# First attention: where DVE takes the second set of side items of a slot, behind one head's thresholds instead of two

## The chip, the cores and the metric

The kernel runs on one core of a Trainium2 chip. Its time is the device time of one launch in microseconds (us), the median over several runs. The engines have a queue each and work in the order in which their instructions are written: PE (TensorE, matmuls), DVE (VectorE), ACT (ScalarE), POOL (GpSimd) and SP (SyncE, which issues DMAs). They meet at semaphores alone.

## The reference, cut to what matters

The program is a two-layer decoder of six stages (three a layer) on x of 8 batches x 256 tokens x 256. The change touches the first stage, an attention with 4 branches of 16 heads of width 16, whose weights are no softmax: softplus of the scaled scores, masked to the past, then w*sigmoid(c*w) (a Silu), then cut off below a threshold of each head, the sink.

```
    Bv, Tv, C = X.shape
    q = (X @ W_Q + b_Q).reshape(Bv, Tv, H_TOT, DH).transpose(0, 2, 1, 3)
    ...
    q, k = (_rope(q), _rope(k))
    scores = jnp.einsum('bhtd,bhsd->bhts', q, k) * ATTNSCALE
    ...
    w = jax.nn.softplus(scores / jnp.sqrt(key_self)[:, :, None, :])
    causal = jnp.tril(jnp.ones((Tv, Tv), bool))
    w = jnp.where(causal, w, 0.0)
    w = w * jax.nn.sigmoid(SCALE * w)
    sinks = sink_scalars.reshape(1, H_TOT, 1, 1)
    w = jnp.where(w < sinks, 0.0, w)
    total = jnp.sum(w, axis=-1, keepdims=True) + sinks + 1e-06
    ...
    y = jnp.einsum('bntc,ncd->bntd', context, W_O) + W_O_bias[None, :, None, :]
    return y.mean(axis=1)
```

## The kernel before

The 16 heads of a batch are worked on in four quads of four heads (each head in all four branches), so the stage has 32 quads, m = 4b + k for batch b and k = 0 to 3. Each engine runs its own loop over slots, one slot for each m (SPAN, a few empty slots ahead and behind), and this order is written out by hand. I call a slot by its k: slot 0 to slot 3 of a batch.

In the slot of quad m the engines do this:

- PE (loop at L417): score groups 1 and 2 of quad m (L346 scores, L349 adds the mask), score group 0 of quad m + 1, the first set of side items, the sums over the weights of quad m - 1 (L366), and the second set of side items.
- ACT (L472): six softplus instructions of quad m, two for each score group (L455); four Silus, one for each head (L484); in between it takes the sums of quad m - 1 out of PSUM (L462) and turned contexts (L469). Each change between softplus and Silu loads a table (L479, L502).
- DVE (L658): takes the first set of side items, cuts the weights of two heads at their thresholds, takes the second set, and cuts the weights of the other two heads. One head is four instructions of 128x384, one for each branch (L654); the last of the sixteen in a slot raises weights_done, for which PE's sums of the next slot wait.
- POOL (L554): adds up rotated queries and keys and finishes contexts behind DVE's items.

The side items are other work that fills the gaps: projections of later batches (q, k, v), the regrouping of sums of quad m - 2, the norm of the keys, the turn of a finished context and the output projection (out). PE computes an item into a PSUM bank, and DVE (ACT for turn) takes it from there. beside_quad (L227) gives both sets of a slot. The second sets, as DVE sees them: slot 0 the out item of batch b - 2 (from batch 2 on), slot 1 one regroup and the keys' projection k of batch b + 1, slot 2 both regroups and q of batch b + 1, slot 3 the other out item of batch b - 1 (from batch 1 on).

PSUM has eight banks. Quad m uses one half of them (banks_of, L222) for its score groups 0 and 2 and the other for group 1; side items and sums of slot m use the half that group 1 of quad m + 1 will write. So the first scores that PE issues in slot m + 1 (L346, by claim at L320) wait until the side items of slot m are taken, the second set too: for an out item by L646, for k and q by L603, for a regroup by L628. DVE's take of an item waits for PE's result of it.

The table that the slots read, in beside_quad; an entry is kind, batch or quad, part and bank:

```
    b, k = divmod(m, QUADS)
    if k == 0:
        sent = [[("regroup", m - 2, 0, 0), ("regroup", m - 2, 1, 1), ("q", b, 2, 2)], [("out", b - 2, 1, 1)]]
    elif k == 1:
        sent = [[("v", b, 0, 0), ("q", b, 3, 1), ("regroup", m - 2, 0, 2)], [("regroup", m - 2, 1, 1), ("k", b + 1, 0, 2)]]
    elif k == 2:
        sent = [[("turn", b - 1, 0, 0), ("turn", b - 1, 1, 1), ("norm", b + 1, 0, 2)],
                [("turn", b - 1, 2, 1), ("turn", b - 1, 3, 2), ("regroup", m - 2, 0, 3), ("regroup", m - 2, 1, 0),
                 ("q", b + 1, 0, 1)]]
    else:
        sent = [[("regroup", m - 2, 0, 0), ("regroup", m - 2, 1, 1), ("q", b + 1, 1, 2)], [("out", b - 1, 0, 1)]]
```

Of the kernel before, what the change touches and what calls it, by code (L numbers as in the profile page):

```python
# [216 lines left out]
def heads_of(k):  # L217

    return slice(8 * (k // 2) + k % 2, 8 * (k // 2) + 8, 2)
# [7 lines left out]
def beside_quad(m):  # L227
# [14 lines that stand above are left out]
    made = lambda kind, of: 0 <= of < (ALL_QUADS if kind == "regroup" else B)  # L242
    return [[(kind, of, i, banks_of(m) + bank) for kind, of, i, bank in part if made(kind, of)] for part in sent]
# [9 lines left out]
def attention0(nc, norm, x_all, xnT_all, ident, psum, a):  # L253
    with ExitStack() as stack:
# [181 lines left out]
        def _(act):  # L436
# [35 lines left out]
            for m in SPAN:  # L472
# [8 lines left out]
                for j in range(4):  # L481
                    if here:
                        wj = w[:, m % QUAD_RING, j].rearrange("p r t -> p (r t)")
                        act.activation(wj, wj, ACT.Silu, scale=SILU_SCALE).then_inc(silu_done, 1)  # L484
                    if j == 0:
                        for _, b, i, bank in turns[:2]:
                            take_turned(b, i, bank)
                    if before and j == (1 if m % QUADS == 2 else 3):
                        for half in range(2):
                            take_sums(m - 1, half)  # L490
                    if j == 1:
                        for _, b, i, bank in turns[2:]:
                            take_turned(b, i, bank)
# [80 lines left out]
        def _(dve):  # L574
# [73 lines left out]
            def threshold(m, j):  # L648

                dve.wait_ge(silu_done, m * 4 + j + 1)  # L650
                for r in range(BR):
                    part = w[:, m % QUAD_RING, j, r, :]
                    col = r * NH + range(NH)[heads_of(m % QUADS)][j]
                    ins = dve.scalar_tensor_tensor(part, part, sinks[:, col:col + 1], part, ALU.is_ge, ALU.mult)  # L654
                if j == 3:
                    ins.then_inc(weights_done, 1)

            for m in SPAN:  # L658
                here = 0 <= m < ALL_QUADS
                first, last = ([item for item in part if item[0] != "turn"] for part in beside_quad(m))  # L660
                for item in first:
                    take(*item)
                for j in range(2):
                    if here:
                        threshold(m, j)
                for item in last:
                    take(*item)
                for j in range(2, 4):
                    if here:
                        threshold(m, j)  # L670

# [1748 lines left out]
```

## Time and profile before

| | us |
|---|---|
| median of 3 runs (lowest to highest) | 2858.23 (2853.45 to 2860.91) |
| the profiled execution's own time | 2861.12 |
| its span, first to last instruction | 2859.1 |
| PE busy | 2470.4 (86%) |
| DVE busy | 1819.9 (64%) |
| ACT busy | 1550.4 (54%) |
| POOL busy | 787.6 (28%) |
| DVE thresholds of the first attention (L654, 512 instructions) | 343.7 |
| ACT softplus (L455, 192) and Silu (L484, 128) | 185.0 and 181.3 |

The profile is of one execution. The first attention takes the span from about 46 us, where its first scores start, to about 704 us, where the last output is added; after that nothing that the change touches runs. Shares of the whole span mix six stages, so the stage is read by itself. A batch in the middle of it (slot 3 of one batch up to slot 2 of the next) takes about 80 us. In a row of the timeline, several like instructions that follow each other stand as one (x8), with their start and the time from the first start to the last end, and in brackets the idle time of the engine ahead of them and what ended it.

### The profile page before, as it was taken

The numbers are of one execution on the slowest core, as the hardware profiler recorded it, in microseconds if no ns is written. First come the engines' busy times: TensorE is split into PE (matmuls) and PEld (weight loads), VectorE is DVE, ScalarE is ACT, GpSimd is POOL, SyncE is SP. The second block draws the span as 40 slices with busy tenths as digits, with TensorE's granted clock in tenths as the row PEclk, the third lists the DMA queues.
The fourth block names the chain that finished last, engine by engine and source line by source line (L and its number), as shares of the span: only waits on it lengthen the run. The fifth ranks groups of instructions, "written<-read, shape, count | busy, mean of one in ns | idle before, by whom it ended". The sixth has DMA issues, their size and how long they took to land. (4 is left out here: it accounts for less than half of the span.)

```text
span 2859.1 us, 46204 instructions
## 1 busy us (share of the span) xinstructions
PE 2470.4 (86%) x17064; PEld 1925.7 (67%) x17064; DVE 1819.9 (64%) x4128; ACT 1550.4 (54%) x3054; POOL 787.6 (28%) x839
## 2 busy tenths in 40 slices
PE   4787878876859999998899999999789999769998
PEld 2444444444646677776688888888767778558887
DVE  5877778775666665554666666666756565455544
ACT  4887878784534444443555555555555555432221
POOL 1332323231014444444211111110036566500000
PEclk8899999888979999999999999999889999979999
DMA  2000000000121111110100000000100000020000
GB/s 90 1 1 1 1 0 1 1 1 20 52 83 27 27 27 28 32 43 4 45 4 6 6 6 3 1 1 1 69 12 5 5 9 1 18 87 8 8 8 30
DMA packets 87052, 55.33 MB, mean 19 GB/s; under 512 B 54960, under 2 KB 78128, under 8 KB 86320
## 3 DMA queue, kind: packets, MB, share of 16 engines
q1 hardware_dynamic: 86832, 52.39, 6.2%
q8 instruction: 139, 2.28, 0.3%
q14 instruction: 81, 0.66, 0.1%
HBM read 37.69 MB, written 8.39 MB: 16 GB/s over the span
## 5 line engine op out<-in xcount | busy, mean ns | idle before, releaser
L654 DVE SCALAR_TENSOR_TENSOR a_w<-a_w,a_sinks 128x384 f32<-128x384 f32 x512 | 343.7, 738 | 10.9 <-ACT a_w L484 9.9
L1991 POOL TENSOR_SCALAR x_weights<-x_weights,x_sums 128x256 f32<-128x256 f32 x256 | 231.9, 924 | 272.5 <-DVE x_sums L2050 272.5
L1083 POOL TENSOR_SCALAR f_weights<-f_weights,f_sums 128x256 f32<-128x256 f32 x256 | 232.0, 924 | 268.5 <-DVE f_sums L1313 268.5
L455 ACT ACTIVATE a_w<-psum 128x1024 f32<-128x1024 f32 x192 | 185.0, 1023 | 124.6 <-PE psum L349 124.2
L346 PE MATMUL psum<-a_qT,a_kT_half 32*128 32x512 f32 x768 | 140.3, 807 | 129.6 <-DVE a_rot L603 36.5
L1241 ACT ACTIVATE f_weights<-psum,f_negmax 128x256 f32<-128x256 f32 x256 | 117.8, 472 | 211.3 <-DVE f_negmax L1307 211.3
L1577 ACT ACTIVATE a_turned_w_hi<-psum 128x512 fp32r<-128x512 f32 x256 | 139.1, 596 | 152.0 <-PE psum L1487 151.9
L1961 ACT ACTIVATE x_weights<-x_masked_s,x_negmax 128x256 f32<-128x256 f32 x256 | 127.0, 497 | 136.5 <-DVE x_negmax L2042 136.5
L1693 DVE TENSOR_REDUCE a_negmax<-psum 128x1 f32<-128x1024 f32 x128 | 156.6, 1224 | 64.8 <-PE psum L119 60.6
L484 ACT ACTIVATE a_w<-a_w 128x1536 f32<-128x1536 f32 x128 | 181.3, 1479 | 0.4
L1655 POOL TENSOR_TENSOR a_xT_lo<-all_xnT_all,a_xT_hi 128x512 fp32r<-128x512 f32 x56 | 71.5, 1276 | 384.8 <-ACT a_xT_hi L1557 384.8
L1700 DVE TENSOR_TENSOR a_turned_w_lo<-psum,a_turned_w_hi 128x512 fp32r<-128x512 f32 x256 | 163.6, 681 | 0.2 <-ACT a_turned_w_hi L1577 0.2
L117 PE MATMUL psum<-a_turned_w_hi,a_v_hi 128*128 128x256 f32 x512 | 150.1, 293 | 0.5 <-DVE a_turned_w_lo L1700 0.5
L346 PEld LDWEIGHTS psum<-a_qT,a_kT_half 32*128 32x128 f32 x768 | 37.4, 224 | 162.1 <-issue 114.6
L118 PE MATMUL psum<-a_turned_w_lo,a_v_hi 128*128 128x256 f32 x512 | 144.8, 283 | 0.0
L119 PE MATMUL psum<-a_turned_w_hi,a_v_lo 128*128 128x256 f32 x512 | 144.8, 283 | 0.0
L1586 ACT ACTIVATE a_weights<-psum,a_negmax 128x1024 f32<-128x1024 f32 x128 | 143.4, 1120 | 2.3 <-DVE a_negmax L1693 2.2
L349 PEld LDWEIGHTS psum<-a_future,a_ident_r 128*128 128x128 f32 x384 | 69.1, 231 | 101.2 <-issue 97.1
L1487 PE MATMUL psum<-all_ident,a_weights 128*128 128x128 f32 x1024 | 132.6, 272 | 0.5 <-ACT a_weights L1586 0.5
L1487 PEld LDWEIGHTS psum<-all_ident,a_weights 128*128 128x128 f32 x1024 | 119.1, 140 | 17.9 <-ACT a_weights L1586 2.2
L544 POOL TENSOR_TENSOR a_ctxn<-a_ctx,a_vnull 128x256 f32<-128x256 f32 x64 | 44.2, 711 | 278.8 <-DVE a_ctx L628 278.8
L117 PE MATMUL psum<-a_kT_hi,a_qT_hi 128*128 128x512 f32 x256 | 106.6, 416 | 7.9 <-issue 6.9
(355 smaller groups left out, 7212.6 us busy)
## 6 DMA issues: line engine op xcount, KB each, us to landing
f_xnT<-all_xnT_all SPq DMA_DIRECT2D x16, 256.0 KB, 2.3
f_pv_rows<-f_pv SPq DMA_DIRECT2D x8, 512.0 KB, 3.2
f_pv_groups<-f_pv_rows SPq DMA_DIRECT2D x8, 512.0 KB
f_w<-in_f_w SPq DMA_DIRECT2D x2, 2048.0 KB, 10.1
all_x_all<-in_x SPq DMA_DIRECT2D x1, 2048.0 KB, 8.3
x_xnT<-all_xnT_all SPq DMA_DIRECT2D x8, 256.0 KB, 2.3
x_ctxT<-in_x_ctxT SPq DMA_DIRECT2D x8, 256.0 KB, 2.9
f_mix_blocks<-f_mix_rows SPq DMA_DIRECT2D x128, 8.0 KB
```

The source lines that it names most:

```text
L117: pe.matmul(out, lhsT[0], rhs[0], start=start, stop=False)
L118: pe.matmul(out, lhsT[0], rhs[1], start=False, stop=False)
L119: return pe.matmul(out, lhsT[1], rhs[0], start=False, stop=stop)
L346: pe.matmul(psum[:, base + j, :], kT_half[rows[j], k % 2, g, keys], at, start=True, stop=False)
L455: act.activation(to, of, ACT.Softplus).then_inc(softened, 1)
L484: act.activation(wj, wj, ACT.Silu, scale=SILU_SCALE).then_inc(silu_done, 1)
L654: ins = dve.scalar_tensor_tensor(part, part, sinks[:, col:col + 1], part, ALU.is_ge, ALU.mult)
L1083: ins = pool.tensor_scalar(w, w, sums[:, k, h, t:t + 1], None, ALU.mult)
L1487: ins = pe.transpose(psum[:, 4 + half, j * P:(j + 1) * P], weights[u % 2][:, lo:lo + P], ident[:])
L1693: dve.tensor_reduce(negmax[:, u % STAT_RING:u % STAT_RING + 1], psum[:, 2 * (u % 2):2 * (u % 2) + 2, :].rearrange("p a n -> p (a n)"), AX. ...
L1700: dve.tensor_tensor(lo, psum[:, 4 + half, :].rearrange("p (j t) -> p j t", t=P), hi.bitcast(F32), ALU.subtract)\
L1991: ins = pool.tensor_scalar(w, w, sums[:, k, h, t:t + 1], None, ALU.mult)
```

## The change

DVE's loop takes the second set of side items behind the thresholds of the first head of a slot, not behind those of the first two. The number of instructions stays the same on every engine, and so does PE's, ACT's and POOL's order.

```
-                for j in range(2):
-                    if here:
-                        threshold(m, j)
+                if here:
+                    threshold(m, 0)
                 for item in last:
                     take(*item)
-                for j in range(2, 4):
+                for j in range(1, 4):
                     if here:
                         threshold(m, j)
```

DVE's order in a slot 1, where the second set is a regroup (L628, L637, L641) and the keys' projection (L598 to L609), before:

```order
L628 COPY a_ctx<-psum 128x4x4x17
L654 SCALAR_TENSOR_TENSOR a_w<-a_w,a_sinks 128x384 x8
L628 COPY a_ctx<-psum 128x4x4x17
L637 TENSOR_TENSOR a_total<-a_ctx,a_sinks_eps 128x4x4 x2
L641 RECIPROCAL a_total<-a_total 128x8x4
L598 STREAM_SHUFFLE a_swap<-psum 128x512
L603 SCALAR_TENSOR_TENSOR a_rot<-psum,a_bk,a_rope 128x256 x2
L609 SCALAR_TENSOR_TENSOR a_rot<-a_swap,a_bk,a_rope 128x256 x2
L654 SCALAR_TENSOR_TENSOR a_w<-a_w,a_sinks 128x384 x8
```

The regroup and the keys come four threshold instructions earlier; twelve follow them instead of eight. Now:

```order
L628 COPY a_ctx<-psum 128x4x4x17
L654 SCALAR_TENSOR_TENSOR a_w<-a_w,a_sinks 128x384 x4
L628 COPY a_ctx<-psum 128x4x4x17
L637 TENSOR_TENSOR a_total<-a_ctx,a_sinks_eps 128x4x4 x2
L641 RECIPROCAL a_total<-a_total 128x8x4
L598 STREAM_SHUFFLE a_swap<-psum 128x512
L603 SCALAR_TENSOR_TENSOR a_rot<-psum,a_bk,a_rope 128x256 x2
L609 SCALAR_TENSOR_TENSOR a_rot<-a_swap,a_bk,a_rope 128x256 x2
L654 SCALAR_TENSOR_TENSOR a_w<-a_w,a_sinks 128x384 x12
```

DVE's order in a slot 0 up to the first item of slot 1 (L617, the values), where the second set is the out item (L646); slot 3 reads alike. Before (-) and now (+):

```order
 L609 SCALAR_TENSOR_TENSOR a_rot<-a_swap,a_bq,a_rope 128x256 x2
-L654 SCALAR_TENSOR_TENSOR a_w<-a_w,a_sinks 128x384 x8
+L654 SCALAR_TENSOR_TENSOR a_w<-a_w,a_sinks 128x384 x4
 L646 SCALAR_TENSOR_TENSOR all_x_all<-psum,all_x_all 128x256
-L654 SCALAR_TENSOR_TENSOR a_w<-a_w,a_sinks 128x384 x8
+L654 SCALAR_TENSOR_TENSOR a_w<-a_w,a_sinks 128x384 x12
 L617 TENSOR_TENSOR a_v<-psum,a_bv 128x16x16 x2
```

The out item moves ahead of the second head's four thresholds.

## Rows read from the trace of the kernel before

**Rows 1.** Windows: stretch, length, busy us (count) of PE, PEld, DVE, ACT, POOL; clock.

```profile
255.63:336.10 80.47, 64.17 (x404) 37.15 (x404) 63.64 (x120) 64.30 (x64) 24.85 (x28) 0.92 0.00 1
```

**Rows 2.** Waits of the stage: who waited for whom, us in total, times, longest.

```profile
PE psum L346 <- DVE a_rot L603: 36.5, 8, 5.1
PE psum L346 <- ACT a_w L455: 32.5, 11, 4.4
PE psum L346 <- issue: 32.5, 14, 2.9
...
PE psum L346 <- DVE all_x_all L646: 14.9, 6, 2.5
...
PE psum L346 <- DVE a_ctx L628: 5.9, 2, 4.7
```

**Rows 3.** Timeline, batch 3, slot 1 into slot 2: start, us, engine, work.

```profile
310.58 1.89 PE L378 MATMUL psum<-all_xnT_all,a_wk 128*128 128x256 f32 x8
...
315.89 0.72 DVE L598 STREAM_SHUFFLE a_swap<-psum 128x512 f32<-128x512 f32 x1
...
317.52 2.09 PE L346 MATMUL psum<-a_qT,a_kT_half 32*128 32x512 f32 x8 [5.05 <-DVE a_rot L603]
318.77 6.11 DVE L654 SCALAR_TENSOR_TENSOR a_w<-a_w,a_sinks 128x384 f32<-128x384 f32 x8
...
320.80 1.94 ACT L455 ACTIVATE a_w<-psum 128x1024 f32<-128x1024 f32 x2 [5.88 <-PE psum L349]
...
327.69 1.50 PE L366 MATMUL psum<-a_w,a_v 128*32 128x512 f32 x16
```

**Rows 4.** Timeline of DVE, cut to the second head's thresholds, slots 0 and 1.

```profile
295.16 2.19 DVE L654 SCALAR_TENSOR_TENSOR a_w<-a_w,a_sinks 128x384 f32<-128x384 f32 x4
...
312.74 2.19 DVE L654 SCALAR_TENSOR_TENSOR a_w<-a_w,a_sinks 128x384 f32<-128x384 f32 x4
```

**Rows 5.** Timeline, slot 3 of batch 2 over slot 0 into slot 1 of batch 3.

```profile
272.40 3.72 PE L414 MATMUL psum<-a_wo,a_ctxT 128*128 128x256 f32 x16
...
277.94 0.41 DVE L646 SCALAR_TENSOR_TENSOR all_x_all<-psum,all_x_all 128x256 f32<-128x256 f32 x1
...
278.61 1.60 PE L346 MATMUL psum<-a_qT,a_kT_half 32*128 32x512 f32 x8 [2.49 <-DVE all_x_all L646]
...
281.40 1.94 ACT L455 ACTIVATE a_w<-psum 128x1024 f32<-128x1024 f32 x2 [3.00 <-PE psum L349]
...
291.17 3.72 PE L414 MATMUL psum<-a_wo,a_ctxT 128*128 128x256 f32 x16
...
292.97 1.06 ACT L462 ACTIVATE a_sumT<-psum 128x512 f32<-128x512 f32 x2
...
297.27 0.41 DVE L646 SCALAR_TENSOR_TENSOR all_x_all<-psum,all_x_all 128x256 f32<-128x256 f32 x1
...
297.79 1.14 PE L346 MATMUL psum<-a_qT,a_kT_half 32*128 32x512 f32 x8 [2.90 <-issue]
...
299.63 1.94 ACT L455 ACTIVATE a_w<-psum 128x1024 f32<-128x1024 f32 x2 [2.35 <-PE psum L349]
```

**Rows 6.** Windows, columns as in Rows 1, scores of four slots' starts.

```profile
278.61:284.21 5.60, 5.60 (x28) 2.54 (x29) 3.97 (x8) 1.94 (x3) 0.00 (x0) 0.70 0.01 3
297.79:301.84 4.05, 4.05 (x28) 1.93 (x28) 4.05 (x8) 1.94 (x2) 0.00 (x0) 1.00 0.00 0
317.52:324.31 6.79, 6.79 (x28) 3.06 (x29) 6.79 (x10) 1.94 (x3) 3.47 (x4) 0.56 0.00 0
398.87:404.09 5.22, 5.22 (x24) 2.43 (x24) 5.22 (x7) 1.94 (x2) 3.47 (x4) 0.70 0.00 0
```

**Rows 7.** Timeline of DVE, start of slot 3 of batch 2.

```profile
267.63 0.88 DVE L628 COPY a_ctx<-psum 128x272 f32<-128x272 f32 x2 [3.50 <-PE psum L399]
```

**Rows 8.** Timeline of PE, the last slot and the tail behind it.

```profile
670.29 3.72 PE L414 MATMUL psum<-a_wo,a_ctxT 128*128 128x256 f32 x16
...
678.76 4.33 PE L366 MATMUL psum<-a_w,a_v 128*32 128x512 f32 x32 [3.87 <-DVE a_w L654]
```

## The prediction, made blind

> **What bounds the kernel now.** I read the stage by itself, first the windows. In a batch of 80.47 us PE is busy 64.17, ACT 64.30 and DVE 63.64 [rows 1]. No engine is full; each idles about 16 us a batch. So the stage is a ring of engines that wait for each other, and what counts is which wait ends last at each change of slot.
>
> The waits name it. PE's first scores of a slot (L346) wait for DVE's take of the keys (L603, eight times, up to 5.1 us), for the out item (L646, six times) and for a regroup (L628, twice) [rows 2]. Fourteen waits are put down to "issue"; six of these are the starts of slot 1 in batches 2 to 7, and there the timeline shows DVE: the out item starts at 297.27, takes 0.41, and PE goes on at 297.79, 0.11 after its end [rows 5]. Behind PE stands ACT: its next softplus (L455) waits 5.88 us after the start of slot 2, 3.00 after that of slot 0, 2.35 after that of slot 1 [rows 3, 5]. A PE start that comes earlier by less than these waits moves ACT by as much, and with ACT everything behind it.
>
> So three of the four slot changes of a batch (0 to 1, 1 to 2, 3 to 0) are set by DVE's take of the second set. The fourth, 2 to 3, is not: PE's second score group there waits for ACT (of the eleven such waits of 32.5 us) [rows 2], so an earlier first group only waits longer.
>
> **What the change does, part by part.** It moves the second set ahead of the second head's four thresholds. These four start at 312.74 in slot 1 and at 295.16 in slot 0, no POOL work beside them [rows 4]. In slot 0 the out item starts at 297.27 [rows 5], so four cost 297.27 - 295.16 = 2.11 us, which is what the item can gain if PE's result is there.
>
> Slot change 1 to 2. The keys' shuffle starts at 315.89; PE's projection lands at 310.58 + 1.89 = 312.47 [rows 3]. 315.89 - 2.11 = 313.78 is later than that, so the whole 2.11 counts. There are eight such changes (in the last batch a regroup alone, which is the 4.7 us wait on L628 [rows 2], moves the same way): 8 x 2.11 = 16.9.
>
> Slot change 0 to 1. PE's output projection lands at 291.17 + 3.72 = 294.89 [rows 5], before 295.16 [rows 4]: again the whole 2.11, six times (batches 2 to 7, since the out item is missing in the first two): 12.7.
>
> Slot change 3 to 0. The out item starts at 277.94, and PE's result lands at 272.40 + 3.72 = 276.12 [rows 5]. Four thresholds earlier would be 275.83; DVE now waits about 0.3 for PE, and the gain is 277.94 - 276.15 = 1.79, six times: 10.7.
>
> Slot 2. No gain, as said. DVE waits for PE's regroup after one head's thresholds, and the four that it had done by then come behind the item, 2.1 us later. DVE's next work, in slot 3, begins after 3.50 us of idle time [rows 7], which hides them with 1.4 left.
>
> The tail. In the last slot PE's output projection lands at 670.29 + 3.72 = 674.01, and PE's sums behind it wait for the last threshold (3.87 us) [rows 8]. DVE now stands at the out item with twelve thresholds undone instead of eight, and nothing follows that could hide them: four more, +2.1 us.
>
> The later weights_done. Of the thresholds' delay, PE's sums of the next slot are what could wait. In slot 1 DVE's work stays the same in sum, so its last threshold still ends 318.77 + 6.11 = 324.88, while PE's sums, at 327.69 [rows 3], come 2.11 earlier: 0.7 us of cover is left. That is the tightest place. If it goes, each further us there is lost again.
>
> These terms sum to 16.9 + 12.7 + 10.7 - 2.1 = 38.2 us.
>
> **The clock.** PE's idle time before these starts also costs speed. From PE's start to ACT's fifth softplus, the start of slot 0 takes 5.60 us at a granted share of 0.70, that of slot 1 4.05 at 1.00 (2.4 GHz throughout; 0.5 is 1.2 GHz) [rows 6]. At the change 3 to 0 PE idles 2.49 before it [rows 5], and with the change 0.7. I take the clock as held there: 1.55 x 6 = 9.3. The bounds are 0 and that. At the change 1 to 2, PE idles 5.05 now [rows 3] and 2.94 then. The start of slot 2 takes 6.79 at 0.56 in batch 3 and 5.22 at 0.70 in batch 4 [rows 6]; at full clock it could take 4.05. The trace shows both outcomes near 2.94: 2.90 at the start of slot 1 leaves the clock whole, 2.49 at slot 0 does not [rows 5, 6]. Bounds: -0.8 on average (if half of the eight are like batch 4's now and all become like batch 3's) to +2.74 each. I take 0.7, since above it PE meets the late weights_done: 8 x 0.7 = 5.6. Both clock terms make 14.9.
>
> The Trainium skill, "TensorE: Matmul & The Clock Gate", section "HAM oscillation — how this bites in real kernels", says that a matmul stream which waits too long between bursts starts each burst at the low clock. By a rule on the length of a wait alone, 2.90 would be cut before 2.49 is; the rows show the reverse, so here the length alone does not decide, and the sum leaves both outcomes open (38 without the clock, 53 with it).
>
> **Sum.** 38.2 + 14.9 = 53.1 us. The profiled execution took 2861.12, so 2808.0; against the median of the runs, 2858.23, it gives 2805.1. I forecast **2805**.
>
> **The rivals.** (1) The clock gives nothing back: the starts stay at their shares of now, and the shift alone counts: 2858.2 - 38.2 = 2820. For it speaks that a start at 0.70 is seen behind 2.49 us of idle time and that the slot 2 to 3 stays cold anyway; against it that only 0.7 us of idle is left ahead of slot 0.
>
> (2) DVE becomes the bound. By the forecast a batch falls by 2.11 + 2.11 + 1.79 + 1.55 + 0.7 = 8.3 to 72.2 us, and DVE's 63.64 [rows 1] are 88% of that, with its short waits for PE still to add. If the changes 0 to 1 and 1 to 2 then pay half, 38.2 - 14.8 = 23.4 is left and no clock: 2835. For it: 0.7 us of cover in slot 1. Against it: DVE has waits of 3 us and more at the head of three slots, such as [rows 7].
>
> (3) No change. PE, freed of DVE, waits for the next thing that holds its banks, ACT's taking of the sums (L462). In slot 0 these end at 292.97 + 1.06 = 294.03, and the out item now ends at 295.57 [rows 5]: 1.5 us too early to bind. It decides if ACT comes that much later against DVE. Then nothing is gained: 2858. The same time follows if occupancy decided, since no engine loses work. The Trainium skill, "Trace Analysis", section "Identifying the Most-Contended Engine", says to take the engine with the highest occupancy as the bottleneck and to work on that first; the change takes no work from any, so by that rule the time would stay. [rows 1] speak against it: the busiest engine is at 80%.
>
> (4) Slower. DVE, in order, stands before a side item that PE has not finished, with three heads' thresholds behind it; weights_done is late, PE's sums wait, ACT waits for the sums, and the slot is longer. The tail shows the price: 2.1 us. It decides where DVE's new wait is longer than the cover, 0.7 us in slot 1. At all 31 later slots it would be +65, 2923; with the gains of the other changes still there, something like a third of that, 2880, is what could happen. The rows give no new wait over 0.3 us in slots 0, 1 and 3, so it is unlikely.
>
> **How the numbers follow.** Forecast 0.70, (1) 0.17, (2) 0.07, (3) 0.04, (4) 0.02. All but the last two are faster by over 0.3% (8.6 us, about what a measurement of this kernel can tell from no change): 0.94, 0.04, 0.02. The range is to hold 8 in 10. Downwards, the slot 2 starts could keep the full clock for part of what lies beyond 0.7 us, some 1.3 more at each of eight: 2805 - 10 = 2795. Upwards it takes in rival (1) and the loss of 0.8 at eight starts, 2820 + 6, and a little of rival (2): 2828.
>
> **What would show it.** Right: PE's waits for L603 fall from about 5.05 to 2.94 each, the waits at the starts of slots 0 and 1 to 0.7 to 0.8; a batch in the middle falls from 80.5 to about 72 us; the window of scores at the start of slot 0 shows 4.05 us at 1.00; the last sums start 2.1 us later against the last out item; the stages behind are unchanged. Rival (1): the same waits, but a batch of 74.5 us. Rival (2): PE's sums (L366) waiting for L654 in slot 2. Rival (3): PE's L346 waiting for L462. Rival (4): DVE waiting for L414 or L378 in the middle of its thresholds for more than 0.7 us. The forecast is wrong in its base if ACT's waits behind PE do not shrink with PE's.

## The result and the profile after

The changed kernel takes 2807.89 us (median of 6 runs, 2803.09 to 2812.0); the kernel before, in runs beside it, 2861.4 (6 runs, 2853.45 to 2863.48). The ratio is 0.9815, with a 95% interval of 0.9801 to 0.9828. That is 53.5 us less; the forecast was 53.1 less, 2805. All times in this document are of fast runs: one of the five runs of the kernel with slot 1 alone (below) took 2931.21 us at a lower granted clock and is left out of its median.

The profiled execution after took 2803.09 us, the shortest of the six. Its page begins so:

```profile
span 2801.1 us, 46204 instructions
...
PE 2450.8 (87%) x17064; PEld 1915.1 (68%) x17064; DVE 1817.3 (65%) x4128; ACT 1551.4 (55%) x3054; POOL 786.4 (28%) x839
```

The counts are those of before: no engine lost an instruction. To see where the time went, one window is laid over the first attention, from its first scores to the last output that DVE adds. The first row is of the kernel before, the second of the kernel after (columns as in [rows 1]: stretch, length, busy us of PE, PEld, DVE, ACT, POOL with counts, then PE's granted clock):

```profile
46.40:704.43 658.03, 517.21 (x3204) 297.19 (x3204) 496.29 (x933) 512.01 (x501) 192.46 (x218) 0.89 0.00 1
```

```profile
44.87:650.03 605.16, 500.29 (x3204) 290.20 (x3204) 493.93 (x933) 512.65 (x501) 191.30 (x218) 0.92 0.00 1
```

The stage is 52.9 us shorter. PE issues the same 3204 matmuls in both, so its part splits cleanly in two. It is idle for 104.9 us instead of 140.8, that is 35.9 less; this is waiting. And it is busy for 16.9 us less with the same work; this is the clock, granted at 0.92 instead of 0.89. Laid against the granted clock, 122.4 us of PE's busy time before were at 1.2 GHz, and 84.4 after; at full speed 38 us of it take half, which is 19 and covers the 16.9. The forecast had 38.2 and 14.9. The other 5.1 us by which the two spans differ lie outside the stage, where nothing was changed.

The waits of the stage after, answering to [rows 2] (who waited for whom, us in total, times, longest):

```profile
ACT a_w L455 <- PE psum L349: 64.5, 54, 8.5
...
PE psum L346 <- ACT a_w L455: 34.9, 10, 4.7
...
PE psum L346 <- DVE a_rot L603: 21.7, 8, 2.9
PE psum L346 <- issue: 18.9, 14, 2.9
PE psum L366 <- DVE a_w L654: 11.4, 9, 4.9
...
PE psum L346 <- DVE all_x_all L646: 4.3, 6, 0.8
...
PE psum L346 <- DVE a_ctx L628: 3.1, 2, 2.6
```

PE's waits for DVE's take fell at every change of slot that the prediction named: for the keys (L603) by 14.8 us, for the out item (L646) by 10.6, under "issue" by 13.6, for the regroup (L628) by 2.8. Of the 13.6, 12.7 are the six starts of slot 1 (from 2.88 to 2.90 each to 0.76 to 0.78), and of the 2.8, 2.1 are the start of slot 2 in the last batch; nearly all of the rest is ahead of slot 3 in batches 0 and 7. ACT's wait for PE fell with them, to 64.5 us; in the kernel before it was:

```profile
ACT a_w L455 <- PE psum L349: 124.2, 54, 9.1
```

One wait is new: PE's sums (L366) for DVE's thresholds (L654), 11.4 us in nine places where there was one of 3.9 [rows 8]. And one is gone. In the kernel before, the sums of slot 2 waited in seven batches for ACT to take turned contexts:

```profile
PE psum L366 <- ACT a_ctxT L469: 4.3, 7, 1.4
```

The change of slot 1 to 2 in batch 3, answering to [rows 3] (start, us, engine, work, and in brackets the idle time ahead and what ended it):

```profile
294.61 1.89 PE L378 MATMUL psum<-all_xnT_all,a_wk 128*128 128x256 f32 x8
...
297.80 0.73 DVE L598 STREAM_SHUFFLE a_swap<-psum 128x512 f32<-128x512 f32 x1
...
299.43 1.69 PE L346 MATMUL psum<-a_qT,a_kT_half 32*128 32x512 f32 x8 [2.94 <-DVE a_rot L603]
300.69 8.22 DVE L654 SCALAR_TENSOR_TENSOR a_w<-a_w,a_sinks 128x384 f32<-128x384 f32 x12
...
302.31 1.94 ACT L455 ACTIVATE a_w<-psum 128x1024 f32<-128x1024 f32 x2 [3.37 <-PE psum L349]
...
308.97 2.93 PE L366 MATMUL psum<-a_w,a_v 128*32 128x512 f32 x32 [0.50 <-DVE a_w L654]
```

Twelve thresholds now follow the keys, the scores wait 2.94 us instead of 5.05, and ACT's softplus waits 3.37 instead of 5.88. The last row shows the later thresholds: PE's sums, which had found the weights ready [rows 3], now wait 0.50 for the last of the twelve. In this place that costs nothing. Before, the second half of the same sums waited as long for ACT:

```profile
329.68 1.50 PE L366 MATMUL psum<-a_w,a_v 128*32 128x512 f32 x16 [0.49 <-ACT a_ctxT L469]
```

From their first start to their end the sums then took 329.68 + 1.50 - 327.69 = 3.49 us; now the wait and the sums make 0.50 + 2.93 = 3.43.

A batch in the middle, answering to [rows 1], and the scores at the starts of slots 0, 1 and 2 of batch 3, answering to [rows 6]:

```profile
240.00:311.72 71.72, 61.41 (x408) 36.13 (x404) 63.36 (x120) 64.34 (x64) 24.68 (x28) 0.95 0.00 1
...
266.32:270.36 4.04, 4.04 (x28) 1.94 (x28) 4.04 (x9) 2.98 (x4) 0.00 (x0) 1.00 0.02 4
281.81:285.87 4.06, 4.06 (x28) 1.94 (x29) 4.06 (x9) 3.58 (x5) 0.00 (x0) 1.00 0.00 0
299.43:305.02 5.59, 5.59 (x28) 2.54 (x28) 5.59 (x7) 1.94 (x2) 3.48 (x4) 0.69 0.00 0
```

The batch is 71.72 us long instead of 80.47 (forecast 72.2), with DVE and ACT as busy as before. The start of slot 0 now runs at the full 2.4 GHz, 4.04 us instead of 5.60. The start of slot 2 still shows 0.69, a mixture of 1.2 and 2.4 GHz.

The tail, answering to [rows 8]: the last out item that DVE takes in the stage's last slot, the thresholds behind it, and PE's last sums.

```profile
615.77 0.42 DVE L646 SCALAR_TENSOR_TENSOR all_x_all<-psum,all_x_all 128x256 f32<-128x256 f32 x1 [1.00 <-PE psum L414]
616.11 6.43 DVE L654 SCALAR_TENSOR_TENSOR a_w<-a_w,a_sinks 128x384 f32<-128x384 f32 x12
...
622.60 5.23 PE L366 MATMUL psum<-a_w,a_v 128*32 128x512 f32 x32 [4.93 <-DVE a_w L654]
```

From the out item to the sums it is 622.60 - 615.77 = 6.83 us. Before, the out item began at 674.05 and the sums at 678.76, which is 4.71: 2.1 more now, as forecast.

### The profile page after: what moved, and what is told of

It is laid out like the page before. It is cut to its first block and busy times, and to the rows that moved or that the text cites. A ratio compares the mean times of both kernels' runs of the same rounds, so it can differ in the third digit from the quotient of the medians.

```text
span 2801.1 us, 46204 instructions
## 1 busy us (share of the span) xinstructions
PE 2450.8 (87%) x17064; PEld 1915.1 (68%) x17064; DVE 1817.3 (65%) x4128; ACT 1551.4 (55%) x3054; POOL 786.4 (28%) x839
## 5 line engine op out<-in xcount | busy, mean ns | idle before, releaser
L654 DVE SCALAR_TENSOR_TENSOR a_w<-a_w,a_sinks 128x384 f32<-128x384 f32 x512 | 343.0, 739 | 3.5 <-ACT a_w L484 3.5
L455 ACT ACTIVATE a_w<-psum 128x1024 f32<-128x1024 f32 x192 | 185.3, 1023 | 65.0 <-PE psum L349 64.5
L346 PE MATMUL psum<-a_qT,a_kT_half 32*128 32x512 f32 x768 | 127.4, 737 | 90.5 <-ACT a_w L455 34.9
L346 PEld LDWEIGHTS psum<-a_qT,a_kT_half 32*128 32x128 f32 x768 | 34.9, 208 | 121.9 <-issue 69.8
L2287 DVE SCALAR_TENSOR_TENSOR f_acc<-psum,f_p,f_acc 128x256 f32<-128x256 f32 x112 | 54.2, 484 | 89.1 <-PE psum L119 85.7
```

The lines of the kernel that those rows point to most:

```text
L346: pe.matmul(psum[:, base + j, :], kT_half[rows[j], k % 2, g, keys], at, start=True, stop=False)
L455: act.activation(to, of, ACT.Softplus).then_inc(softened, 1)
```

## The experiments

Apart from the fillers below, all of them edit one place, DVE's loop. It thresholds some heads, takes the second set, and thresholds the other heads:

```
+                ahead = <number of heads>
+                for j in range(ahead):
-                for j in range(2):
                     if here:
                         threshold(m, j)
                 for item in last:
                     take(*item)
-                for j in range(2, 4):
+                for j in range(ahead, 4):
```

The kernel before is 2 in every slot, the change is 1 in every slot. In this table a ratio is to the kernel before on the same chip, with its interval. Gains in us are told below as this ratio's share of 2861, since the medians come from several chips and go apart by some us. PE's idle and busy time are of one profiled execution, over the stage as above, less those of before. The forecast's terms, with the same signs, stand in the last column (idle, busy).

| heads ahead of the second set | us | ratio | idle | busy | forecast |
|---|---|---|---|---|---|
| 1 in slot 1 (e1_again) | 2850.79 | 0.9964 (0.9945 to 0.9984) | -12.0 | +1.9 | -16.9, -5.6 |
| 1 in slot 0 (e2_slot0) | 2851.68 | 0.9963 (0.9948 to 0.9978) | -11.8 | -0.3 | -12.7, 0 |
| 1 in slot 3 but the last (e3_slot3) | 2842.86 | 0.9931 (0.9916 to 0.9946) | -11.0 | -7.0 | -10.7, -9.3 |
| 1 in slot 2 (e4_slot2) | 2862.66 | 1.0004 (0.9995 to 1.0014) | +1.2 | -4.3 | 0, 0 |
| 1 in slots 0 and 3 (e10_slots03) | 2832.05 | 0.989 (0.9874 to 0.9907) | -23.1 | -7.3 | -23.4, -9.3 |
| 1 in slots 0, 1 and 3 (e5_013) | 2803.96 | 0.9805 (0.9788 to 0.9821) | -37.8 | -22.5 | -40.3, -14.9 |
| 1 everywhere (the change) | 2807.89 | 0.9815 (0.9801 to 0.9828) | -35.9 | -16.9 | -38.2, -14.9 |
| 0 everywhere (e6_none) | 2823.11 | 0.9867 (0.9849 to 0.9885) | -24.6 | -14.4 | |
| 3 everywhere (e7_three) | 2920.89 | 1.0207 (1.0192 to 1.0222) | +46.2 | +12.6 | |

Lengths of slots, where they are given below, run from ACT's fifth softplus in the slot before to ACT's fifth softplus in the slot itself, so that the wait ahead of a slot's start and that start count as this slot's; sums are over all batches.

How far one execution's clock can be trusted shows in the row of slot 2: the medians are the same, and yet its profiled stage is 3.0 us shorter, with 4.3 of busy time. So a few us of busy time mean nothing here.

### One change of slot at a time

Slot 1 alone:

```
+                ahead = 1 if m % QUADS == 1 else 2
```

> The move in slot 1 of each batch alone (regroup and keys ahead of the second head's thresholds); slots 0, 2 and 3 as before. Theory (the slot changes pay one by one, and the gains add): eight changes of 2.11 us, 16.9, and up to 7 more from the clock at the start of slot 2, so 17 to 24 us less than before, about 2840. PE's wait for L603 falls from 5.05 to 2.94. Rival (the ring takes the gain back elsewhere as long as one slot alone is moved, since another wait comes to stand in its place): under 5 us.

Measured: 2852.16 us (median of 4), ratio 0.9965 (0.995 to 0.9981), about 10 us less, and so too little. The same kernel was run again for its trace.

> The move in slot 1 alone once more, for a profile and a second time: the first gave 10 us (ratio 0.9965), less than the 17 to 24 that were expected, and its profile was of a disturbed run. Theory 1 (the shift of 2.11 us pays eight times, but the clock at the starts of slots 2 and 0 falls otherwise than it did and takes some back): PE's wait for L603 is 2.94 in each batch, the lengths of slot 1 to slot 2 fall by 2.1 or more, and other slot lengths grow. Theory 2 (the shift itself does not pay, PE's sums in slot 2 meet the late thresholds): PE's L366 waits for L654 by about 2 us in slot 2 of each batch. The time again about 2851.

Measured: 2850.79, again about 10 us less. The first two rows are the stage and the start of slot 1 in batch 3, then the starts of slots 2 and 3 in batch 4:

```profile
46.39:694.28 647.89, 519.07 (x3204) 297.89 (x3204) 494.53 (x933) 513.19 (x501) 192.71 (x218) 0.89 0.00 1
```

```profile
295.18:302.15 6.97, 6.97 (x28) 3.19 (x30) 4.12 (x8) 1.95 (x3) 0.00 (x0) 0.54 0.00 0
395.18:399.24 4.06, 4.06 (x28) 1.94 (x29) 4.06 (x5) 1.95 (x3) 3.23 (x4) 1.00 0.00 0
412.77:422.09 9.32, 6.13 (x28) 2.73 (x28) 7.75 (x10) 6.90 (x8) 5.00 (x5) 0.58 0.00 0
```

PE's waits for the keys did fall to 2.93 each, as worked out, and slots 2 are together 24.6 us shorter. But slots 1 are 7.4 longer and slots 3 are 7.7 longer. In three batches the start of slot 1, which took 4.05 before, is now slow (6.97 at 0.54 in batch 3). And where the start of slot 2 runs at the full clock, as in batch 4, the sums meet DVE's late thresholds: PE waits 2.03 us for them in batches 2, 4 and 6, and the start of slot 3 behind them takes 9.32 us at 0.58. So the wait was shortened, but the clock only changed its place, and where a start of slot 2 was fast the cover in slot 1 gave out. The length of the wait does not tell which start is slow: behind the same 2.93 us slot 2 takes 4.06 in batch 4 and 6.95 in batch 3.

Slot 0 alone, and slot 3 alone (without the last slot of all, so that the tail stays):

```
+                ahead = 1 if m % QUADS == 0 else 2
```

> The move in slot 0 of each batch alone (the out item ahead of the second head's thresholds). Theory: six changes of 2.11 us, 12.7 in all, no term of the clock, since the start of slot 1 runs at a share of 1.00 already: about 2849. PE's wait at the start of slot 1 falls from 2.90 to 0.78. Rival (the gain is taken back elsewhere): under 5 us.

Measured: 2851.68 us, about 10.6 less; 11.8 us of idle time are gone and the clock is as it was. The shift is worth what its term said, within 1 to 2 us.

```
+                ahead = 1 if m % QUADS == 3 and m < ALL_QUADS - 1 else 2
```

> The move in slot 3 of each batch alone, the very last slot left as before. Theory: six changes of 1.79 us, 10.7, and six times 1.55 us because the start of the next slot 0 keeps the full clock (5.60 us becomes 4.05): 20.0 in all, about 2841. Rival 1 (the clock gives nothing): 10.7, about 2851, and the window stays at 5.6. Rival 2 (taken back elsewhere): under 5 us.

Measured: 2842.86, about 20 less, as expected. The rows are the starts of slots 0 and 1 of batch 3:

```profile
274.41:278.47 4.06, 4.06 (x28) 1.94 (x28) 4.06 (x9) 3.52 (x4) 0.00 (x0) 1.00 0.02 4
292.03:296.07 4.04, 4.04 (x28) 1.94 (x29) 4.04 (x8) 1.95 (x3) 0.00 (x0) 1.00 0.00 0
```

Slot 0 now starts at full clock behind 0.7 us of idle time, in all six batches, and slot 1 keeps it behind 2.88 in five of them; in batch 6 it starts at 0.69 (5.59 us) behind 2.90. Both terms of this change of slot, shift and clock, came in, less those 1.5 us.

Slot 2 alone:

```
+                ahead = 1 if m % QUADS == 2 else 2
```

> The move in slot 2 alone. Theory (PE's second score group of slot 3 waits for ACT there, so an earlier or later take of the queries moves nothing, and the later thresholds are hidden by 3.5 us of idle time of DVE): no change, 2861, within 3. Rival (the later thresholds or DVE's wait for the regroup cost): 2866 or more.

Measured: 2862.66, ratio 1.0004 (0.9995 to 1.0014): no change. The change of slot 2 to 3 is not set by DVE.

### The changes of slot together

```
+                ahead = 1 if m % QUADS in (0, 3) and m < ALL_QUADS - 1 else 2
```

> The move in slots 0 and 3, not in slots 1 and 2, the very last slot as before. Alone they paid 10.6 and 19.7 us, slot 1 alone 10; all three 57 or so. So some 17 us belong to moves that stand together. Theory (clock: a start that keeps its clock sends the low clock on to the next start that waits long; with slots 0 and 3 moved those starts wait 0.8 us and cannot take it, so slot 1 pays its full 17 to 24 only on top of them): 12.7 + 20.0 = 32 us here, about 2830, and the change adds 24 to that. Rival (slots 0 and 3 help each other, slot 1 pays 10 in any company): 45 us, about 2817.

Measured: 2832.05, about 31 less, the sum of the two alone (10.6 + 19.7). Idle time adds up too: 23.1 against 11.8 + 11.0.

```
+                ahead = 2 if m % QUADS == 2 or m == ALL_QUADS - 1 else 1
```

> The changed kernel with slot 2 and the very last slot as before (second set behind two heads there). Theory: slot 2's move pays nothing and costs nothing, so its return changes nothing; the last slot gives back the 2.1 us of the tail: 2806 against 2808 for the change, a ratio of about 0.981. Rival (slot 2's move has its part in the gain, through DVE's earlier take of the queries): 2812 or more. Second rival (slot 2's move costs, its thresholds being late for PE's sums): under 2803.

Measured: 2803.96, a ratio of 0.9805 where 0.981 was expected. It keeps the changes that pay and leaves out the tail's 2.1 us. The intervals of the two ratios (0.9788 to 0.9821 here, 0.9801 to 0.9828 for the change) overlap, so that it is better than the change is not shown, though it is the fastest of the runs.

What the prediction did not have comes out of the pair. With slots 0 and 3 moved, slot 1 is worth (0.989 - 0.9805) x 2861 = 24 us; alone it was worth 10. The three alone make 10.3 + 10.6 + 19.7 = 40.6 us, together they make about 56. The idle time explains little of that: 12.0 + 11.8 + 11.0 = 34.8 alone, 37.8 together. The busy time explains it: 5.4 us in sum alone, 22.5 together. So the shifts add up, and the clock does not. The expectation of the kernel with slots 0 and 3 had this; its rival, that slot 1 pays 10 us in any company, is out. Busy time at 1.2 GHz, of one execution each, says the same: 122 us before, 127 with slot 1 alone, 107 with slot 3 alone, 105 with slots 0 and 3, 72 with all three.

### The clock by itself

These kernels leave DVE's order alone and give PE something to do ahead of a start: extra matmuls into a bank that the coming scores overwrite, whose results nobody reads. Ahead of slot 0, on the kernel before:

```
                 first, last = beside_quad(m)
+                if here and m % QUADS == 0 and m >= 8:
+                    bank = banks_of(m - 1) + 2
+                    pe.wait_ge(*free[bank])
+                    for _ in range(9):
+                        pe.matmul(psum[:, bank, 0:T], same_head[:], xnT_all[:, 0, 0, :], start=True, stop=True)
```

> The kernel before, with nine extra matmuls of 128x256 (about 2.1 us) that PE does in its idle 2.49 us ahead of slot 0 from batch 2 on, into a PSUM bank that is free then; their result is overwritten. DVE's order is as before, so PE's wait for the out item ends when it did and nothing is shifted. Theory (the idle time there costs clock as well as time): the start of slot 0 takes 4.05 us instead of 5.60 at a granted share of 1.00, six times 1.55 = 9.3 us less, about 2852. Rival (the low clock at this place lies beside other work and costs nothing, or goes on for another reason): no change, 2861.

Measured: 2863.62, ratio 1.0011 (0.9998 to 1.0024). This one was mis-sized: the nine took 3.87 us instead of fitting into the 2.49 us of idle time, and held the scores back by about 1.4, so its time says nothing of the clock. Its trace says one thing: slot 0 starts at full clock in all six batches, and slot 1 is slow behind it in two of them (6.91 and 6.83 us) and fast in four. The filler in batch 3:

```profile
280.28 4.05 PE L424 MATMUL psum<-all_xnT_all,a_same_head 128*128 128x256 f32 x18
```

With five in place of nine:

```
-                    for _ in range(9):
+                    for _ in range(5):
```

> As e8_fill0, with five extra matmuls instead of nine (nine took 3.87 us, not 2.1, and so held back the scores of slot 0 by some 1.4 us each). Five take about 2.15 of the 2.49 us that PE idles. Theory (the idle time ahead of slot 0 costs clock as well): the start of slot 0 takes 4.05 us at full clock at its old place, 6 x 1.55 = 9.3 us less, about 2852. Rival (the low clock there costs nothing on the path): 2861.

Measured: 2860.4, ratio 0.9997 (0.9985 to 1.0008): nothing gained, where 9.3 us were expected. The starts of slots 0 and 1 of batch 3:

```profile
280.61:284.65 4.04, 4.04 (x28) 1.94 (x29) 3.97 (x8) 1.95 (x3) 0.00 (x0) 1.00 0.02 4
298.22:303.81 5.59, 5.59 (x28) 2.54 (x29) 4.12 (x8) 1.94 (x3) 0.00 (x0) 0.69 0.00 0
```

The filler did what it should: slot 0 starts at full clock in all six batches, and slots 0 are 10.8 us shorter. But now slot 1 starts at 0.69 in all six, 5.59 us instead of 4.05; slots 1 are 7.4 longer, and the rest is 2.9 longer. Keeping one start at speed moved the slow start to the next long wait. The term "1.55 x 6" of the prediction is therefore not had by a fast start of slot 0 alone. (The filler is more work for PE, too; no run tells apart whether slot 1 is slow for this work or for the wait.)

Ahead of slot 2, on top of the change:

```
+                if here and m % QUADS == 2 and m >= 2:
+                    bank = banks_of(m - 1) + 3
+                    pe.wait_ge(*free[bank])
+                    for _ in range(6):
+                        pe.matmul(psum[:, bank, 0:T], same_head[:], xnT_all[:, 0, 0, :], start=True, stop=True)
```

> The changed kernel with six extra matmuls (about 2.6 us) in the 2.94 us that PE still idles ahead of slot 2, into a bank that is free then; the result is overwritten. It keeps the clock at the start of slot 2 without shifting PE's start. Theory (the weights' cover is used up: PE's sums in slot 2 already wait 0.5 us for DVE's last threshold, so an earlier ACT meets PE's later sums): the start of slot 2 falls from 5.59 to 4.05 us, PE's wait for L654 in slot 2 grows from 0.5 to about 2 us, and the time falls by less than 4 us, 2804 or more. Rival (the clock is what still costs there): 8 x 1.55 = 12 us less, 2796.

Measured: 2815.95, ratio 0.9848 (0.9831 to 0.9865), about 9 us slower than the change by the ratios. The expectation had up to 4 us of gain and no loss. The start of slot 2 and the sums of that slot in batch 3 as windows, and the sums and ACT's taking of them in the timeline (lines are 5 higher here, so L659 is the threshold):

```profile
301.40:305.46 4.06, 4.06 (x28) 1.94 (x28) 4.06 (x5) 1.94 (x2) 3.23 (x4) 1.00 0.01 4
310.95:315.41 4.46, 4.46 (x33) 1.31 (x34) 2.65 (x5) 2.19 (x3) 0.00 (x0) 0.62 0.00 0
```

```profile
310.95 4.46 PE L366 MATMUL psum<-a_w,a_v 128*32 128x512 f32 x32 [2.04 <-DVE a_w L659]
...
313.80 0.60 ACT L467 ACTIVATE a_sumT<-psum 128x512 f32<-128x512 f32 x1 [1.25 <-PE psum L366]
```

The start gains 5.59 - 4.06 = 1.53 us, and 2.04 - 0.50 = 1.54 of it comes back as waiting for the last threshold. Behind that longer wait the sums run at 0.62, 4.46 us instead of 2.93, and slot 3 is over 3 us longer. In batch 1 the sums keep the full clock, and there slots 2 and 3 together take as long as with the change, within 0.3 us. So the cap that the prediction put on slot 2 is real: a faster start of slot 2 is worth nothing once DVE's thresholds are what the sums wait for, and less than nothing when the wait costs the clock.

### How many heads ahead

```
+                ahead = 0
```

> The second set ahead of all thresholds, in every slot. Theory (from one head to none PE's results are not there yet): DVE waits about 3.9 us for the output projection in slots 3 and 0 (0.3 and 0 behind one head), 1.8 for the keys in slot 1; some of it is won back as POOL's work falls into the wait and no longer beside thresholds; DVE has no slack left at the change 3 to 0 and 1.3 us at 0 to 1; the tail is 2 us longer. 17 to 37 us slower than the change: 2825 to 2845. Rival (only PE's release counts, so earlier is always better): 2806 or less.

Measured: 2823.11, ratio 0.9867 (0.9849 to 0.9885), 15 us slower than the change. The waits of its stage, then DVE at the change of slot 0 to 1 in batch 3:

```profile
DVE all_x_all L646 <- PE psum L414: 64.5, 16, 11.8
...
PE psum L366 <- DVE a_w L654: 36.0, 9, 8.1
...
PE psum L346 <- DVE a_rot L603: 13.4, 8, 1.7
```

```profile
284.10 0.42 DVE L646 SCALAR_TENSOR_TENSOR all_x_all<-psum,all_x_all 128x256 f32<-128x256 f32 x1 [2.24 <-PE psum L414]
284.44 8.54 DVE L654 SCALAR_TENSOR_TENSOR a_w<-a_w,a_sinks 128x384 f32<-128x384 f32 x16
```

This is the slower rival at work: DVE stands before an out item that PE has not finished, 2.24 us here and 3.85 at the change of slot 3 to 0 before it, with all sixteen thresholds behind it, and PE's sums wait 36.0 us for thresholds instead of 11.4. (Of the 64.5 us in the first row, 21.3 are the end of the stage; with the change the row has 25.8 in all.) The time came out a little below the expected range, and the loss was not where it was expected. Slots 0 and 1 are about as long as with the change, and slots 2 are shorter, by 18 us; the late thresholds are paid in slots 3, which are 30 us longer (24.4 to 26.2 us each in batches 1 to 6, where the change has about 21).

```
+                ahead = 3
```

> The second set behind three heads, in every slot: the change turned round. Theory (DVE's take sets three of four slot changes): 20 changes of 2.11 us, 42 us slower than before, and 0 to 20 more as the longer idle times cost clock: 2903 to 2923. Rival (the waits lie beside ACT's work and DVE's order matters only where it is short): under 2880.

Measured: 2920.89, ratio 1.0207 (1.0192 to 1.0222), 60 us more, as expected.

```profile
PE psum L346 <- issue: 67.1, 14, 5.0
...
PE psum L346 <- DVE a_rot L603: 51.3, 8, 7.2
...
PE psum L346 <- DVE all_x_all L646: 27.6, 6, 4.6
```

One head is again about 2.1 us at each of the three changes of slot: the keys' wait is up to 7.2, the out item's to 4.6, the start of slot 1's to 5.0. Slot 2 to 3 costs nothing again. With 0, 1, 2 and 3 heads ahead the kernel takes 2823, 2808, 2861 and 2921 us: each head is worth 50 to 60 us until the thresholds behind become late.

## Why the prediction was right, and where it was not

**The ring and its waits: right.** No engine was full, and the time was in the waits that end last at three of the four changes of slot. Each of the three pays by itself, and slot 2 pays nothing. The rival by occupancy is out: DVE is as busy as before in the stage, and the kernel is 1.85% faster. The kernel with no head ahead turns it round: DVE is less busy there than in any other (463.7 us of the stage against 493.9 after the change) and the kernel is slower than the change.

**The shift, 38.2 us: right within 2.3.** Of PE's idle time 35.9 went. Change by change the waits did what their terms said: at 1 to 2 they fell by 14.8 + 2.1 = 16.9 (forecast 16.9), at 0 to 1 by 12.7 (12.7), at 3 to 0 by 10.6 (10.7), and 1.6 more went where none was named, nearly all of it ahead of two starts of slot 3. That makes 41.8. The later thresholds took 7.5 of it back (11.4 against 3.9), the tail included. The prediction priced the tail at 2.1, which it is, and took the cover in slot 1 as just enough. In eight places it was not quite: 0.42 to 0.52 in six batches, 1.60 in batch 0, 1.88 in the last. Two things it had not seen: the 4.3 us of waiting for ACT's turned contexts went in the same places, and PE's second score groups wait 2.4 more for ACT (34.9 against 32.5). With these, 41.8 - 7.5 + 4.3 - 2.4 = 36.2, all but 0.3 of what was measured.

**The clock, 14.9 us: the size is right, one reason is not.** PE is busy for 16.9 us less. By place, six starts of slot 0 gain 1.54 each, 9.2, as forecast; the starts of slot 2 fell from about 6.2 us in the mean to 5.2, where 0.7 each was forecast. But the prediction treated these as gains of their places: less idle time ahead of slot 0, so a fast start of slot 0. The filler of five ahead of slot 0 shows that this is not enough, since the slow start then moves to slot 1 and nothing is gained. And with slots 0 and 3 moved but not slot 1, busy time falls by 7.3; with slot 1 as well, by 22.5. My reading is that the low clock falls on one of the long waits that are left in the batch, and that the gain comes from there being fewer of them: after the change the waits ahead of slots 0 and 1 are 0.7 to 0.8 us, and only those ahead of slot 2 (2.94) and, for ACT, inside slot 3 (up to 4.7) are long. The runs agree with this, but they don't show by which rule it falls on one wait and not on another. In the kernel with slot 3 alone, slot 1 starts at full clock behind 2.88 us in five batches of six; in the one with five matmuls ahead of slot 0, at 0.69 behind 2.88 to 2.90 in all six; in the one with nine, slow in two. That stays open.

**The sum: within 0.4 us, in part by luck.** The shift came out 2.3 us below its term and the clock 2.0 above, so the two misses cancel; the six executions of the changed kernel spread over 9 us, and the one in which the parts were read is 4.8 below their median, with 5.1 us of its gain outside the stage.

**The cap on slot 2: there, but it did not set the 0.7.** The prediction took 0.7 us a slot because more would meet the late thresholds. In the six middle batches the starts of slot 2 gained 0.69 in the mean (from 6.28 to 5.59), but it is the clock, 0.69 in each of them, that ended the gain there, while the 0.50 us that the sums wait for thresholds took the place of 0.49 for ACT. So the size came in by luck. That the cap lies close behind, the filler ahead of slot 2 shows: it gave 1.53 more and lost all of it.

**Batch 0: not forecast.** In the profile after, the sums of slot 2 in batch 0 wait 1.60 us and then run slowly, 4.48 us instead of 2.93, and ACT, which takes them out, waits:

```profile
91.47 4.48 PE L366 MATMUL psum<-a_w,a_v 128*32 128x512 f32 x32 [1.60 <-DVE a_w L654]
...
94.16 0.60 ACT L462 ACTIVATE a_sumT<-psum 128x512 f32<-128x512 f32 x1 [1.36 <-PE psum L366]
```

Slot 3 of that batch is 4.4 us longer than before. In the kernel with slots 0, 1 and 3 moved the same sums wait as long and run at full speed:

```profile
92.16 2.79 PE L366 MATMUL psum<-a_w,a_v 128*32 128x512 f32 x32 [1.63 <-DVE a_w L654]
```

So the wait belongs to the order, and the slow sums behind it come or not with the clock; with slot 1 alone they came as well (4.48 us behind 1.63). It is one reason why the profiled stage of the kernel with three slots moved is shorter than the change's.

**The rivals.** That the clock gives nothing (2820) is out by PE's busy time. That DVE becomes the bound (2835) is out, though its sign, sums that wait for L654 in slot 2, is there at 0.5 us: what comes in this place beyond that wait would be lost, as the kernels with the second filler and with no head ahead show. No change (2858) and slower are out for this change; slower is what the step after it begins to be.

## What to carry to other kernels

Where several engines wait for each other and none is full, list for each handover which wait ends last; moving a take ahead of work that nobody waits for yet is worth that work's time at every such handover, and these shifts add up. Ask in the same breath who waits for the work that was pushed back, and by how much it was early: here one head's thresholds were paid for by that margin, and two were not. A gain in clock, on the other hand, is not to be booked place by place: test it with all the long waits in view, since a slow start that is cured in one place can turn up at the next.

## What the runs showed of the hardware

**The granted clock does not follow from the wait ahead.** The same 2.88 us of idle time came with a start at full clock (4.04 us) and with one at 0.69 (5.59 us), in one kernel the same 2.93 us with 4.06 and 6.95, and the same 1.6 us with sums of 2.79 and of 4.48 us. Nor is a slow start always slow from its beginning. In the kernel before, the start of slot 0 in batch 3 [rows 6] runs at full clock for its first 0.54 us, behind 2.49 us of waiting, and falls to 1.2 GHz only then:

```profile
278.61:279.15 0.54, 0.54 (x5) 0.31 (x8) 0.54 (x2) 0.00 (x0) 0.00 (x0) 1.00 0.00 0
279.15:281.40 2.25, 2.25 (x16) 1.03 (x8) 2.25 (x5) 0.00 (x0) 0.00 (x0) 0.50 0.03 7
```

The Trainium skill, "TensorE: Matmul & The Clock Gate", section "HAM oscillation — how this bites in real kernels", describes bursts that all start cold because each wait before them is too long. The rows agree that PE falls to 1.2 GHz beside its waits, and waits of 0.7 us ahead of slots 0 and 1 never came with it here; they do not agree with a rule on the length of one wait, nor with a start that is slow from its first matmul.

**DVE's thresholds are dearer beside POOL.** With no head ahead all sixteen stand in one block, as in slot 0 of batch 3, where POOL had no instruction from 284.63 to 296.60: 8.54 us, 0.53 each. After the change the twelve behind the keys, with POOL's work on the keys beside them, took 8.22, 0.69 each. Over the whole stage after the change, the 134 thresholds that overlap an instruction of POOL last 1.11 us in the mean, the other 378 last 0.61. Over the stage of the kernel with no head ahead the 512 thresholds are 32 us cheaper than after the change:

```profile
L654 DVE SCALAR_TENSOR_TENSOR a_w<-a_w,a_sinks 128x384 f32<-128x384 f32 x512 | 311.0, 680 | 0.0
```

```profile
L654 DVE SCALAR_TENSOR_TENSOR a_w<-a_w,a_sinks 128x384 f32<-128x384 f32 x512 | 343.0, 739 | 3.5 <-ACT a_w L484 3.5
```

The first row is of that kernel, the second of the change (busy us and mean ns of one behind the bar). The Trainium skill, "SBUF — State Buffer", section "Who interferes with whom", says that a DVE instruction with two inputs in SBUF contends with a GpSimd instruction that reads SBUF; these rows agree. And the 32 us bought nothing, since DVE waited longer for PE instead.

**A matmul of 128x256 in f32 stands in the trace as two.** The filler of nine shows 18 records 0.215 us apart (the row with L424 above), 3.87 us at that pace; that doubling is why it was too long.
